# Two layers of attention and expert mixing on one core: the weighted mix moves from TensorE to three other engines, the routing has fewer steps, the order of all calls is new

## The reference

```python
x = x + attention(norm(x), ctx, w0, bias0, mask0)        # 16 heads of 8, 77 keys, bias [4,16,512,77]
x = x + first_ffn(norm(x))                                # 8 experts, top 2, capacity 64, 128 -> 512 (GELU) -> 128
x = x + attention(norm(x), ctx, w1, bias1)
x = x + second_ffn(norm(x))                               # 8 real and 2 null experts, top 2, 128 -> 128 plus bias

# first_ffn, per group of 256 tokens
probs = softmax(xg @ w_router);  top 2 of probs; first choices queue ahead of second ones
a token's place in its expert's queue = running count; kept if it is at most 64
out = sum over its kept choices of probs[e] * expert_e(token)

# second_ffn
probs = softmax(x @ gate_w.T + gate_b);  weights, selected = top_k(probs, 2)
weights of null experts become 0;  norm_w = weights / sum(weights)  (sum 0 is taken as 1)
out[t] = sum over e of norm_w[t, e] * (x[t] @ expert_w[e] + expert_b[e])
```

## Time and profile before

| | |
|---|---|
| median of three runs | 356.58 us (353.12 to 357.16) |
| the profiled execution's own time | 353.75 us |
| its span, from first to last instruction | 352.0 us |
| mean granted clock of TensorE | 0.982 of full speed |
| instructions | 9050 |

### The profile page before, as it was taken

One profiled execution on the slowest core, in us unless ns is written; L12 is line 12 of the kernel. 1 busy time (PEld: TensorE's weight loads), 2 busy tenths in 40 slices (PEclk: granted clock), 3 DMA queues, 4 the chain that ended last, 5 costly groups with the idle time before them and its releaser, 6 DMA issues.

```text
span 352.0 us, 9050 instructions
## 1 busy us (share of the span) xinstructions
PE 302.5 (86%) x3633; PEld 227.6 (65%) x3633; DVE 237.1 (67%) x555; ACT 194.3 (55%) x369; POOL 216.7 (62%) x238
## 2 busy tenths in 40 slices
PE   2788979979999999997999988998779898988970
PEld 1467666747896878685877767864558465846620
DVE  4487777997587769836799853577278755644361
ACT  2163545519493498566997467944756264432231
POOL 7277565687370889277928688559993487245115
PEclk9999989999999999998999999999999999999996
DMA  6996990505001510101000011011000000010000
GB/s 184 256 359 171 309 271 5 154 2 155 17 15 41 165 32 32 33 25 39 31 4 15 17 32 48 33 40 37 2 2 0 32 3 2 0 34 0 2 30 31
DMA packets 29757, 23.37 MB, mean 66 GB/s; under 512 B 2741, under 2 KB 27155, under 8 KB 29715
## 3 DMA queue, kind: packets, MB, share of 16 engines
q1 hardware_dynamic: 28691, 20.68, 20.6%
q0 software_dynamic: 1024, 2.10, 2.2%
HBM read 19.63 MB, written 3.15 MB: 65 GB/s over the span
## 4 chain that ended last, share of the span: by engine, by line
PE 31%; POOL 22%; issue 16%; ACT 14%; DVE 13%; DMA 2%; POOLq 0%; DVEq 0%; ACTq 0%
POOL shared L536 6%; POOL SC L474 5%; PE HBK L1342 5%; PE EBK L1354 4%; PE SP L1174 4%; PE PB L1193 4%; PE HBK L1280 3%; ACT PT L743 3%; PE SP L1155 3%; DVE SC L1774 2%; ACT SC L735 2%; POOL DG L509 2%; DVE mx L1776 2%; ACT a_xn L723 2%; DMA shared<-slab,rows 2%
## 5 line engine op out<-in xcount | busy, mean ns | idle before, releaser
L474 POOL TENSOR_TENSOR SC<-SC,mx 128x1232 f32<-128x1232 f32 x32 | 72.4, 2264 | 43.4 <-DVE mx L1776 43.3
L735 ACT ACTIVATE SC<-SC 128x1232 f32<-128x1232 f32 x32 | 39.5, 1237 | 30.6 <-POOL SC L474 30.6
L743 ACT COPY PT<-SP 128x512 f32<-128x512 f32 (+1 forms) x96 | 43.4, 524 | 9.9 <-PE SP L1174 9.6
L536 POOL DMA_INDIRECT shared<-slab,rows x32 | 33.1, 1034 | 23.3 <-DMA slab<-W 14.5
L1776 DVE TENSOR_REDUCE mx<-SC 128x16 f32<-128x1232 f32 x32 | 46.0, 1436 | 1.1
L1174 PE MATMUL SP<-ident,SC 128*128 128x128 f32 x320 | 41.8, 277 | 4.4 <-ACT SC L735 3.4
L1174 PEld LDWEIGHTS SP<-ident,SC 128*128 128x128 f32 x320 | 35.8, 142 | 9.5 <-ACT SC L735 5.1
L1280 PE MATMUL HBK<-ein,wi_s 128*128 128x128 f32 x256 | 36.6, 287 | 4.4 <-ACT hT L760 4.4
L1774 DVE TENSOR_TENSOR SC<-SP,amp 128x1232 f32<-128x1232 f32 x16 | 23.0, 1437 | 23.8 <-PE SP L1155 23.8
L1280 PEld LDWEIGHTS HBK<-ein,wi_s 128*128 128x128 f32 x256 | 32.1, 196 | 9.3 <-ACT hT L760 8.2
L1781 DVE RECIPROCAL rc<-PB 128x128 f32<-128x128 f32 x32 | 30.4, 951 | 9.7 <-PE PB L1193 9.7
(11 more groups left out here) (198 smaller groups left out, 559.5 us busy)
## 6 DMA issues: line engine op xcount, KB each, us to landing
BI<-in_fside_Bx16xSxS SPq DMA_DIRECT2D x8, 1232.0 KB, 6.9
wi_s<-in_L_ffn_wi SPq DMA_DIRECT2D x1, 2048.0 KB, 10.2
slab<-W SPq DMA_DIRECT2D x16, 128.0 KB, 1.7
X<-in_x SPq DMA_DIRECT2D x4, 256.0 KB, 4.3
out<-acc SPq DMA_DIRECT2D x3, 256.0 KB, 2.1
MI<-in_mask_BxSxS_ik SPq DMA_DIRECT2D x8, 77.0 KB, 6.8
ew_s<-in_L_ffn_expert_w SPq DMA_DIRECT2D x1, 512.0 KB, 5.1
shared<-slab,rows POOLq DMA_INDIRECT x32, 2.6
```

The costliest lines, as they stand in the source:

```text
L474: g.tensor_tensor(S4, S4, m4, ALU.subtract).then_inc(s["shifted"], 1)
L536: g.indirect_dma_start(out=G[:, i, k, :], out_offset=None, in_=slab, in_offset=bass.IndirectOffsetOnAxis(ap=rows[:, i, k:k + 1], axis=0), ...
L735: sc.activation(S3, S3, ACT.Exp).then_inc(s["probs"], 1)
L743: sc.copy(PT[:, c0:c1, :].rearrange("p c t -> p (c t)"), SP[:, n, 0:(c1 - c0) * P]).then_inc(s["PTs"], 1)
```

## The change

The mix of runs 4 to 6 is done as run 7's was: copy_experts, spread_weights, mix and finish are gone with their buffers Y and DG. The first four experts of a tile go to bank HBK, the other four to EBK, after start_acc has taken the bias out of EBK; weigh_expert takes HBK on DVE, scale_experts EBK on ACT, sum_experts adds on POOL. acc exists once, so start_acc of runs 5 and 6 waits for the store of the run before. Run 7 is done as before.

Routing compares exponentials that are not divided by their sum. The first choice is where logits minus maximum is zero, so it needs neither exponential nor sum; the second is the maximum of the exponentials without the first. Sum and reciprocal are needed for the gates of layer 0 alone and move out of the chain (own semaphores m_gate and m_row), layer 1 normalises by its kept sum as before. The chain to positions has 11 steps for 16, layer 0's routing 21 instructions in all for 23, layer 1's 18 for 24.

All five lists of calls are in a new order: almost every call of a tile stands in the list as before, at other places between its neighbours.

```diff
-    ROUTE0, ROUTE1 = 23, 24
+    ROUTE0, ROUTE1 = 13, 18
...
             if f < 2 * B - 1:
-                return HBK[:], HBK[:]
+                return HBK[:], EBK[:]
...
             def store(b):
-                sp.wait_ge(s["n_out"], b + 1)
+                sp.wait_ge(s["n_done"], NT * (b + 1))
...
-            def spread_weights(f, i):
...
             def sum_experts(f, i):
-                pool.wait_ge(s["n_scaled"], i + 1)
-                if i > 0:
-                    pool.wait_ge(s["n_done"], i)
+                n = NT * batch_of(f) + i
+                pool.wait_ge(s["n_scaled"], n + 1)
+                if n > 0:
+                    pool.wait_ge(s["n_done"], n)
...
-            def copy_experts(f, i, n):
...
             def experts(f, i):
                 m = batch_of(f)
                 for n in range(2):
-                    t = 2 * (NT * m + i) + n
-                    if f < 2 * B - 1 or 2 * i + n == 0:
-                        if i == 0 and n == 0 and layer_of(f - 1) == 0:
-                            pe.wait_ge(s["m_hs"], NE * mixtures_before(f))
-                        if t > 0:
-                            pe.wait_ge(s["n_copied"], t)
+                    if f < 2 * B - 1:
+                        if i == 0:
+                            pe.wait_ge(s["n_acc"], m + 1)
+                        else:
+                            pe.wait_ge(s[("n_used", "n_scaled")[n]], NT * m + i)
+                    elif 2 * i + n == 0:
+                        pe.wait_ge(s["n_used"], NT * m)
...
-            def mix(f, i):
...
             def ranked(f, c):
+                if c == 0:
+                    step(f, v.scalar_tensor_tensor(r_k[:, :, 0:width(f)], r_l[:, :, 0:width(f)], 0.0, ranks,
+                                                   ALU.is_equal, ALU.mult))
+                else:
+                    step(f, v.tensor_tensor(r_k[:, :, 0:width(f)], r_q[:, :, 0:width(f)], ranks, ALU.mult))
...
             def without_first(f):
+                routed(f, layer_of(f) + 5)
+                dve.wait_ge(s["n_exp" if layer_of(f) else "m_exp"], batch_of(f) + 1)
+                step(f, v.scalar_tensor_tensor(r_p[:, :, 0:width(f)], chosen(f, 0), -2.0, r_e[:, :, 0:width(f)],
+                                               ALU.mult, ALU.add))
...
+            def second_gate(f):
+                dve.wait_ge(s["m_gate"], 4 * batch_of(f) + 2)
+                routed(f, 7)
+                v.tensor_tensor(r_g[:, :, 1], r_m1[:], r_g[:, :, 0], ALU.mult).then_inc(s["m_gate"], 1)
...
             def divisor(f):
+                routed(f, 15)
+                step(f, v.scalar_tensor_tensor(r_r[:], r_s[:], 0.0, r_s[:], ALU.is_le, ALU.add))
...
             def start_acc(f):
                 m = batch_of(f)
                 dve.wait_ge(s["n_bias"], m + 1)
+                xo = sl(X, m).rearrange("p o i d -> p (o i d)")
+                if f == 2 * B - 1:
+                    for i in range(NT):
+                        dve.wait_ge(s[f"l_sum{i}"], 1)
+                    xo = acc[:].rearrange("p i d -> p (i d)")
+                elif m > 0:
+                    dve.wait_ge(s["st_out"], 16 * m)
                 v.tensor_tensor(acc[:].rearrange("p i d -> p (i d)"), EBK[:], xo, ALU.add).then_inc(s["n_acc"], 1)
-
-            def finish(f):
...
```

More of the change, by code:

```diff
@@ L1344, in experts @@
                               start=True, stop=True).then_inc(s["n_eo"], 1)
-            def mix(f, i):
-                t = NT * batch_of(f) + i
-                if i == 0:
-                    pe.wait_ge(s["n_bias"], batch_of(f) + 1)
-                pe.wait_ge(s["n_copied"], 2 * t + 2)
-                pe.wait_ge(s["n_diag"], 2 * t + 2)
-                for e in range(NE):
-                    last = te.matmul(EBK[:, i * D:(i + 1) * D], DG[i % 2][:, e, :], Y[i % 2][:, e, :],
-                                     start=False, stop=(e == NE - 1), skip_group_check=True)
-                last.then_inc(s["n_mix"], 1)
+            turn_weights((0, 1), "ld_wa", 0)
             turn_ctx()
-            turn_weights((0, 1), "ld_wa", 0)
             a_xTr(0)
@@ L1481, in _ @@
+            attn_scores(3, 3, 0)
+            weigh_values(3, 1)
+            down(1, 1)
+            turn(3, 2, 0)
+            turn(3, 2, 1)
+            project(3, 1, 0)
+            a_xTr(4)
+            up(1, 5)
+            weigh_values(3, 2)
+            query(4, 1)
+            turn(3, 3, 0)
+            turn(3, 3, 1)
+            up(1, 6)
+            attn_scores(4, 0, 1)
+            project(3, 2, 0)
+            up(1, 7)
+            attn_scores(4, 1, 1)
             down(1, 2)
-            weigh_values(3, 1)
@@ L1525, in _ @@
             turn(4, 2, 1)
[L1526 to L1532 removed]
+            up(2, 6)
+            project(4, 1, 1)
+            positions(3)
+            turn(4, 3, 0)
+            a_xTr(5)
+            weigh_values(4, 2)
+            query(5, 1)
+            turn(4, 3, 1)
+            up(2, 7)
             project(4, 2, 1)
@@ L2111, in _ @@
             pick(1, 1)
+            invert(2, 0)
+            normalise(2, 0)
+            softmax_max(2, 2, 0)
+            gates(0)
+            own_position(1)
+            position(1)
+            slot(1)
+            exp_sum(1)
+            slots(1, 0)
+            slots(1, 1)
+            add_residual(2, 0, 0)
+            softmax_max(2, 3, 0)
+            invert(2, 1)
+            normalise(2, 1)
+            add_residual(2, 1, 0)
             invert(2, 2)
+            within(1)
+            scale_q(3, 0)
@@ L2150, in _ @@
-            is_best(2, 1)
-            invert(3, 1)
+            best(2)
+            is_best(2)
             ranked(2, 1)
+            invert(3, 2)
+            normalise(3, 2)
             first_best(2, 1)
             pick(2, 1)
-            normalise(3, 1)
+            scale_q(4, 1)
+            softmax_max(4, 0, 1)
+            second_gate(2)
+            add_residual(3, 2, 0)
+            softmax_max(4, 1, 1)
             own_position(2)
+            invert(3, 3)
+            normalise(3, 3)
@@ L2194, in _ @@
             without_first(3)
-            best(3, 1)
-            is_best(3, 1)
+            best(3)
+            gates(2)
+            is_best(3)
             ranked(3, 1)
             first_best(3, 1)
-            softmax_max(4, 3, 1)
             pick(3, 1)
-            invert(4, 1)
-            normalise(4, 1)
             own_position(3)
+            position(3)
+            within(3)
             slot(3)
```

1076 lines of the change are left out of this document (496 added, 580 removed).

## The result

The changed kernel takes 345.22 us (median of four runs: three from 343.83 to 345.52, and one of 353.91 in a slower state of the chip); the kernel before took 355.25 in the same series. The ratio is 0.971 with an interval of 0.962 to 0.979; a second series gave 344.71 and 0.973 (0.969 to 0.977). It is faster, by 9 to 10 us; 342 was forecast. The profiled execution took 343.83 us, span 342.1, 9.9 less than before.

What follows compares the result with a forecast made beforehand. The prediction took PE's chain to bound the late stretch, with DVE slightly busier after the change. Gains of 9.8 + 2.8 + 1.8 = 14.4 us gave 342 from the median of 356.58; range 328 to 355, the forecast's own 333 to 351.

Steps and rivals of the forecast that it cites:

- the main term: Run 6's first transpose to the last logits, 249 to 330.3: from 81.3 to 71.5 us, a gain of 9.8.
- the term in front of it: Before run 6's first transpose: shifts ahead of the gathers and DG gone from POOL, 0 to 5.6 us, 2.8 taken.
- What bounds: Before, PE by its chain from 268 to 330.3; after, DVE busier at 62.4 us against PE's 59.6 in the stretch.
- The floor of the stretch is 62.4: 249 to 330.3: DVE's busy sum as floor, plus the 9.1 us PE leaves unused today, gives 71.5.
- gathers later mean batch 3's second attention later: POOL before run 6's first transpose: reason to take no more than 2.8 us of a possible 5.6.
- Tail, 1.8: Behind the last logits: the last tile's mix leaves PE ahead of run 7's experts, a gain of 1.8 us.
- Routing and the part up to 235: Shorter routing and new order before 235 us: counted as 0, with 4 us either way.
- a sign that the order and not the mix is the cause: A stage before 235 us moving by more than 4 us would show the forecast wrong.
- Costs per instruction: Runs 4 to 6: multiply-adds 0.375 us each on DVE, four scalings 1.1 on ACT, three additions 1.64 on POOL.
- Waits and store: PE waits nothing to 0.5 us a tile if DVE is at hand; start_acc's store wait costed at nothing, else 3.7 twice.
- The slower one, 368: Expert banks lock PE to DVE's queue behind softmax_max pairs: twelve waits of 2.9 us, 35 against 23.8 gained; chance 0.12.
- PE was not the wall: PE had slack by its load row and DVE's added 16 us bind at once: no change, 352; chance 0.20.

Runs made afterwards that it cites:

- the runs with 6.7 and 6.6 us less: Changed kernel with 24 multiply-adds fewer on DVE, 344.27 us; changed kernel with expert matmuls of runs 4 to 6 cut to half their columns, 347.66 us.
- the last run: Against the version with old order up to 235, new behind and gathers moved (341.76 us): every remaining link before run 7's scores moved up; 343.20 us.

## Why the prediction was right, and where it was not

The time came out inside the range in part by luck: the main term gave 2.3 of its 9.8 us, the term in front of it 5.7 for 2.8, and the new order behind run 6's first transposes, on which the gain turned out to hang, was in no term of the sum.

**What bounds.** Before: PE by its chain. That part was not tested alone. After: the forecast said the busier engine, DVE with 62.4 us, and left 9.1 us unused behind it. DVE came to 64.6 and PE to 65.9 (59.6 was forecast), the gap to 13.1, and neither sum sets the length, as the runs with 6.7 and 6.6 us less show. The step that failed is to build the stretch from a busy sum: "The floor of the stretch is 62.4", with today's unused time added. What is left to bound it is the sequence of waits between the engines, and of the changes that were made only the late part of the order moved it: 77.2 us with the new functions in the old order, 65.4 in the new one. That no single engine's work does so was tested engine by engine, the sequence itself is the conclusion from it.

**The main term, 9.8.** Measured 2.3 for the stretch as I cut it. By the change without its order it is zero (0.9999). I costed the freed PE time as if the order could not give it away; the old order did so, with idle time of PE (14.0 us between run 7's first softmax and last logits, 7.3 in the new order) and with the lower clock.

**Before it, 2.8.** 5.7, just above the upper bound of 5.6. Of these, 3.8 are the step that was forecast, 3.6 from the first softmax to the first transpose by the shifts ahead of the gathers (249.1 - 237.8 before, 243.3 - 235.8 after); the other 2.0 are run 6's earlier start, which the routing alone gives too (1.8) and the forecast counted as nothing. The reason for the discount was true, "gathers later mean batch 3's second attention later": add_mixture(3) came 5.2 later (257.0 to 262.3) and run 7 1.7 later.

**Tail, 1.8.** 1.9; but not for any order, as the old one shows (21.5 us).

**Routing and the part up to 235, 0 with 4 either way.** Routing alone is 1.5 in its own run. Run 6's first softmax came at 235.8 for 237.8. Stages before that moved by more than 4 us (first softmax of run 4 by 14.3 to the front, mixture(1) by 10.3 to the back), which I had named as a sign that the order and not the mix is the cause. The sign was right in its conclusion, not in its place: the early order is neutral and the late one decides.

**Costs per instruction.** The multiply-adds were priced well: 0.346 mean and, four in a row on one tile, 0.38 apart (289.87, 290.25), 0.375 forecast. So were ACT and POOL (0.370; 0.73 + 0.48 + 0.46 = 1.67 a tile). DVE's busy sum rose by 18.4, not 11: the routing steps that lasted more than 0.33 us hold 25.2 us beyond 0.2 each, 11.5 before; most end with a POOL instruction. PE's fell by 12.8, not 23: 22 us of the sum after lie in stretches at half clock, 6.4 of the sum before, so that by an estimate from these two some 8 us came back as longer matmuls; the other 2 or 3 stay open. The groups of scalings and multiply-adds on the page after (busy, mean ns of one, idle before), as the earlier trace rows:

```profile
L775 ACT ACTIVATE weighed<-EBK,cw 128x128 f32<-128x128 f32 x52 | 14.8, 370 | 14.7 <-PE EBK L1315 11.2
...
L1955 DVE SCALAR_TENSOR_TENSOR acc<-HBK,cw,acc 128x128 f32<-128x128 f32 x51 | 17.7, 346 | 5.0 <-PE HBK L1315 3.8
```

**Waits and store.** HBK and EBK cost PE under 1 us a tile, as forecast, but as a property of the new order. start_acc never waited for a store; run 7's first multiply-add still did, 1.1 us for 2.10. Timeline of DVE after:

```profile
286.41 0.69 DVE L1936 TENSOR_TENSOR acc<-EBK,X 128x512 f32<-128x512 f32 x1 [0.68 <-PE EBK L1294]
...
289.87 0.73 DVE L1955 SCALAR_TENSOR_TENSOR acc<-HBK,cw,acc 128x128 f32<-128x128 f32 x2
...
328.39 0.35 DVE L1955 SCALAR_TENSOR_TENSOR acc<-HBK,cw,X 128x128 f32<-128x128 f32 x1 [1.12 <-DMA out<-acc]
```

**Rivals.** The slower one, 368, was a mechanism of the old order with the new functions, 8.0 us in all for HBK and start_acc where the mix was exchanged alone; with the other waits and the clock it cost the gain and no more. "PE was not the wall" gave 352, near the 353.86 that the change without its order takes. The Trainium skill ("Perfetto Trace Analysis", "Identifying the Most-Contended Engine") warns against matmul busy time as a measure of how near TensorE is to its limit; the run with half the expert columns agrees: 6.6 us less of it, and no less time.

**Open.** The late order with the old mix on TensorE was not run, so how much of the 11.6 us the new mix makes possible is not known, only that it gives none without that order.

## What to carry to other kernels

Before costing the removal of work from an engine by busy sums, ask what its place in the list will hold afterwards: work that went to another engine comes back as a wait where nothing stands between two uses of a bank. Look for the bound by taking work away from one engine at a time; where no engine's work moves the end, as here, suspect the sequence, and cost a change of the mix and its order as one. Measure a new order from the point that feeds the end (here run 7's first softmax) and behind it, not by total busy time: in the last run that point came 6.2 us sooner, and the rest grew by 8.

## What the runs showed of the hardware that I had not expected

A small DVE instruction with two SBUF inputs stands still while POOL reads and writes SBUF, and the profile counts it as busy: 1.43 and 2.02 us for 0.20, ending 0.06 us behind POOL's. A reduction with one input beside the same POOL instruction took 0.20, and multiply-adds that read PSUM 0.35 as ever. The Trainium skill ("SBUF — State Buffer", "SBUF: two separate sides") says that such an instruction and a GpSimd one that reads SBUF exclude each other for the whole instruction; the traces agree.

Where TensorE's work was cut or delayed, its granted clock was lower (0.91 for 0.96 with half the expert columns, 0.53 for 0.85 over 21.9 us in the last run), and part of what was cut came back as longer matmuls: with half the columns, two pairs at half clock took 1.06 and 1.22 us, for 0.59 to 0.70 elsewhere.
